# Four graph layers on one core: the bias of two banks written by ScalarE instead of PE, a copy moved to GpSimd, and a new order of the edge stages

## The reference, cut to what matters

```python
hi = x @ W1[:H];  hj = x @ W1[H:]
h = relu(hi[:, :, None, :] + hj[:, None, :, :] + b1)
y = h @ W2 + b2
y = layernorm(y) * gamma + beta
out = einsum('bij,bijh->bih', adj, y)
```

## Time and profile before

| | |
|---|---|
| median of 3 runs | 458.41 us (458.27 to 459.51) |
| profiled execution (the page gives its span) | 459.2 us |
| PE busy | 440.2 us, 96% |
| DVE busy | 416.2 us, 91% |
| ACT busy | 386.5 us, 84% |
| POOL busy | 354.0 us, 77% |
| granted TensorE clock, mean | 0.987 |

### The profile page before, as it was taken

The page is one execution under the profiler, slowest core; times in us unless marked ns, Lnnn a source line. Parts: engine busy times, 40 slices in busy tenths (PEclk is TensorE's granted clock), DMA queues, the critical chain, the costliest instruction groups (busy, mean ns, idle before and its releaser), DMA issues. The chain is left out here.

```text
span 459.2 us, 14175 instructions
## 1 busy us (share of the span) xinstructions
PE 440.2 (96%) x3420; PEld 414.6 (90%) x3453; DVE 416.2 (91%) x1523; ACT 386.5 (84%) x1003; POOL 354.0 (77%) x651
## 2 busy tenths in 40 slices
PE   8699989999999999999999999999999999999993
PEld 3599989999999999889998999999999999999991
DVE  6989999999999999996898898899889888989975
ACT  2368979999999899998788888888888888888874
POOL 4569979999999899756677787777768676868762
PEclk9889999999999999999999999999999999999997
DMA  7134344445444652233313222232223131313111
GB/s 221 41 83 131 95 139 161 153 151 178 154 148 156 221 190 77 76 109 121 122 55 99 69 74 80 69 85 63 91 60 94 51 103 51 103 51 86 37 46 49
DMA packets 50939, 47.60 MB, mean 104 GB/s; under 512 B 5584, under 2 KB 42576, under 8 KB 50896
## 3 DMA queue, kind: packets, MB, share of 16 engines
q1 hardware_dynamic: 49760, 46.45, 33.2%
q10 hardware_dynamic: 1136, 0.66, 0.5%
HBM read 28.22 MB, written 18.87 MB: 103 GB/s over the span
## 5 line engine op out<-in xcount | busy, mean ns | idle before, releaser
L1593 PEld LDWEIGHTS bank<-w2c,hE 128*128 128x128 f32 x512 | 67.3, 192 | 2.4
L1593 PE MATMUL bank<-w2c,hE 128*128 128x128 f32 x512 | 67.5, 275 | 0.2
L905 ACT ACTIVATE hE<-bank,front 128x512 f32<-128x512 f32 x64 | 44.2, 691 | 7.6 <-PE bank L1574 7.4
L927 ACT ACTIVATE sqE<-bank 128x512 f32<-128x512 f32 x63 | 37.7, 599 | 12.8 <-PE bank L1593 12.3
L1237 DVE TENSOR_REDUCE ssum<-sqE 128x4 f32<-128x512 f32 x63 | 42.6, 676 | 4.3 <-ACT sqE L927 2.9
L706 POOL TENSOR_TENSOR gHl<-gH,gHu 128x512 fp32r<-128x512 f32 x32 | 41.0, 1283 | 5.6 <-ACT gHu L879 5.6
L1104 DVE BATCH_NORM_STATS2 stats<-t 128x6 f32<-128x128 f32 x192 | 44.4, 272 | 1.0 <-issue 1.0
L1262 DVE TENSOR_TENSOR ym<-bank,wE 128x512 f32<-128x512 f32 x64 | 43.2, 681 | 1.6 <-POOL wE L755 0.3
L722 POOL TENSOR_TENSOR half<-ym 128x512 f32<-128x512 f32 x31 | 39.5, 1273 | 3.3 <-DVE ym L1262 3.1
L1591 PE MATMUL bank<-bias,ones_b 128*128 128x512 bf16 x92 | 35.0, 380 | 0.7 <-DVE ym L1262 0.6
L1593 PEld LDWEIGHTS bank<-w2c,hC 128*128 128x128 f32 x256 | 33.6, 192 | 1.3
(11 more groups left out here) (191 smaller groups left out, 1624.6 us busy)
## 6 DMA issues: line engine op xcount, KB each, us to landing
hh_scratch<-hh SPq DMA_DIRECT2D x32, 256.0 KB, 2.2
gH<-hh_scratch SPq DMA_DIRECT2D x32, 256.0 KB, 2.8
A<-adj_groups SPq DMA_DIRECT2D x32, 128.0 KB, 2.1
res_scratch<-res SPq DMA_DIRECT2D x32, 128.0 KB, 2.1
gRES<-res_scratch SPq DMA_DIRECT2D x32, 128.0 KB, 2.5
AT<-adjT_groups SPq DMA_DIRECT2D x31, 128.0 KB, 2.3
out<-y SPq DMA_DIRECT2D x30, 128.0 KB, 1.9
X<-x_groups SPq DMA_DIRECT2D x29, 128.0 KB, 2.2
```

The costliest lines, as they stand in the source:

```text
L905: nc.scalar.activation(hE[g][:, :], HE_ps, ACT.Relu, bias=C["L3_b1"]).then_inc(b[f"hE{g}_ready"], 1)
L927: nc.scalar.activation(sqE[g][:, :, :], YE_ps[g], ACT.Square).then_inc(b[f"sqE{g}_ready"], 1)
L1593: last = nc.tensor.matmul(ps[:, i, :], hidden[:, i * P:(i + 1) * P], w2c[:, :], start=False, stop=i == tiles - 1)
```

## The change

1. ScalarE writes the bias. For every unit but the first, a new stage `seed_ell(g)` (`sd0`, `sd1`) copies the centred bias row, repeated four times, into the bank of m0 or m1 as soon as `x0` or `x1` of the unit before has read it. `project` then leaves its product of ones and bias out, and its four products add to what is there. m0 and m1 wait for the seed instead of for `ymE0`, `ymE1`. `mc` keeps its product.
2. `split_upper` leaves ScalarE. GpSimd's `add_ends` (`hs`) does it as a `tensor_copy` behind its sum, and waits for one semaphore more (`HC_psum` of two units before).
3. SP's `next_h` is placed by `spl` alone. Its waits are as before.
4. `T3` and `FIRST` are new, `FIRST` now for units 0 to 7. The constants (`PERIOD3`, `AGES`, `START3`) are as before.

```diff
-        T3 = {"idx": 0, "T": 2.44, "spu": 3.82, "hs": 6.51, "beg": 7.08, "Qp": 7.27, "rows": 8.02, "spl": 8.21, "kS": 11.23, "V": 11.89,
-              "g0": 12.34, "T2": 14.04, "r0": 14.78, "cols": 15.16, "gc": 15.34, "kST": 15.55, "g1": 15.81, "rc": 16.63, "r1": 17.9,
-              "m0": 18.3, "mc": 19.24, "s0": 19.26, "m1": 19.31, "sqc": 20.27, "d0": 20.97, "s1": 21.21, "dc": 21.5, "d1": 23.51,
-              "std": 23.58, "rec": 24.31, "w": 25.33, "x0": 25.58, "yn": 25.84, "x1": 25.92, "a1": 28.54, "a2": 29.78, "sc": 31.11,
-              "tot": 33.56, "gm": 33.91, "rs": 34.76, "st": 35.78, "ag": 37.68, "fstd": 38.76, "frec": 41.49, "om": 43.47, "sh": 46.57,
-              "app": 49.01}
+        T3 = {"idx": 11.83, "rows": 19.84, "V": 25.63, "cols": 27.21, "g0": 24.24, "g1": 26.7, "gc": 27.9, "m0": 28.45, "m1": 32.1, "mc": 30.82,
+              "sc": 43.04, "Qp": 15.42, "kS": 18.49, "kST": 23.94, "r0": 21.32, "r1": 24.83, "rc": 24.3, "sd0": 24.05, "sd1": 25.41, "s0": 26.02,
+              "s1": 29.14, "sqc": 29.1, "std": 29.77, "fstd": 45.76, "app": 56.37, "beg": 16.18, "T": 11.05, "T2": 22.48, "d0": 28.62, "d1": 30.77,
+              "dc": 30.14, "rec": 32.25, "x0": 32.94, "x1": 34.86, "yn": 34.7, "tot": 41.42, "st": 44.67, "ag": 44.82, "frec": 53.11, "spl": 13.44,
+              "hs": 10.29, "a1": 33.48, "a2": 37.09, "gm": 39.87, "rs": 41.67, "w": 30.03, "om": 46.9, "sh": 50.85}
...
-            edge_stages = [(("idx", 0.5), next_ot), (("spl", "hs", 1.5), next_h), (("rs", 0.8), next_res), (("app", 1), store)]
+            edge_stages = [(("idx", 0.5), next_ot), (("spl", 1.5), next_h), (("rs", 0.8), next_res), (("app", 1), store)]
...
                 wait_past(pool, b["HE1_psum"], count(2))
+                wait_past(pool, b["HC_psum"], count(2))
                 nc.gpsimd.tensor_tensor(hs[q][:, :, :], gH[q][:, :, 0:P], gH[q][:, :, P:2 * P], ALU.add).then_inc(b["hs_ready"], 1)
+                nc.gpsimd.tensor_copy(gHu[q][:, :, :], gH[q][:, :, :]).then_inc(b["split_up"], 1)
...
-            def split_upper(q, u, count):
-
-                act.wait_ge(gh_loaded[q], (u - q) * 8 + 16)
-                wait_past(act, b["HE1_psum"], count(2))
-                wait_past(act, b["HC_psum"], count(2))
-                nc.scalar.activation(gHu[q][:, :, :], gH[q][:, :, :], ACT.Copy).then_inc(b["split_up"], 1)
...
+            def seed_ell(g):
+                def stage(q, u, count):
+                    if isinstance(u, int) and u == 0:
+                        return
+                    act.wait_ge(b[f"ymE{g}_ready"], count(1))
+                    nc.scalar.activation(YE_ps[g], b2c[:, :].unsqueeze(1).to_broadcast([P, ELL, P]), ACT.Copy).then_inc(b[f"seedE{g}_done"], 1)
+                return stage
...
-            edge_stages = [("spu", split_upper), ("Qp", keep_Q), ("kS", keep_S), ("kST", keep_ST), ("r0", hidden_ell(0)),
-                      ("r1", hidden_ell(1)), ("rc", hidden_csr), ("s0", square_ell(0)), ("s1", square_ell(1)),
+            edge_stages = [("Qp", keep_Q), ("kS", keep_S), ("kST", keep_ST), ("r0", hidden_ell(0)),
+                      ("r1", hidden_ell(1)), ("rc", hidden_csr), ("sd0", seed_ell(0)), ("sd1", seed_ell(1)), ("s0", square_ell(0)), ("s1", square_ell(1)),
...
-            def project(ps, hidden, tiles, done):
-                nc.tensor.matmul(run(ps), ones_b[:, :], run(bias3[:, :, :]), start=True, stop=False)
+            def project(ps, hidden, tiles, done, seeded=False):
+                if not seeded:
+                    nc.tensor.matmul(run(ps), ones_b[:, :], run(bias3[:, :, :]), start=True, stop=False)
...
-                    wait_past(pe, b[f"ymE{g}_ready"], count(1))
-                    project(YE_ps[g], hE[g], ELL, f"YE{g}_psum")
+                    seeded = not (isinstance(u, int) and u == 0)
+                    if seeded:
+                        pe.wait_ge(b[f"seedE{g}_done"], count(1))
+                    else:
+                        wait_past(pe, b[f"ymE{g}_ready"], count(1))
+                    project(YE_ps[g], hE[g], ELL, f"YE{g}_psum", seeded)
```

More of the change, by code:

```diff
@@ L305, in gnn_stack @@
                   "esd_ready", "erstd_ready", "wE_ready", "ymE0_ready", "ymE1_ready", "yC_ready", "O_psum", "half_done", "accE_ready",
[L306 removed]
+                  "tot_ready", "gout_done", "tout_ready", "ostats_done", "omv_ready", "omean_ready", "ostd_ready", "orstd_done", "oshift_ready", "out_ready", "seedE0_done", "seedE1_done"]
         b = {n: sem("u_" + n) for n in names3}
@@ L364, in wait_past @@
                 engine.wait_ge(semaphore, n)
-        T3 = {"idx": 0, "T": 2.44, "spu": 3.82, "hs": 6.51, "beg": 7.08, "Qp": 7.27, "rows": 8.02, "spl": 8.21, "kS": 11.23, "V": 11.89,
[4 rows of a table removed]
-              "app": 49.01}
+        T3 = {"idx": 11.83, "rows": 19.84, "V": 25.63, "cols": 27.21, "g0": 24.24, "g1": 26.7, "gc": 27.9, "m0": 28.45, "m1": 32.1, "mc": 30.82,
[4 rows of a table added]
         AGES = 4
         START3, EARLY, CATCH = 216.0, 5.0, 25.0
[L376 to L380, removed]
[7 rows of a table removed]
-                 ("beg", 2): 225.69, ("beg", 3): 240.58, ("beg", 4): 244.47, ("beg", 5): 247.21, ("rows", 0): 219.62, ("rows", 1): 225.56,
-                 ("rows", 2): 229.73, ("rows", 3): 243.06, ("rows", 4): 251.45, ("rows", 5): 263.45, ("s1", 0): 220.31, ("s1", 1): 234.83,
[4 rows of a table removed]
-                 ("cols", 0): 223.8, ("cols", 1): 228.19, ("cols", 2): 236.96, ("cols", 3): 246.55, ("cols", 4): 261.85, ("cols", 5): 272.97,
-                 ("gc", 0): 224.76, ("gc", 1): 229.1, ("gc", 2): 238.28, ("gc", 3): 247.38, ("gc", 4): 261.99, ("gc", 5): 274.28, ("kST", 0): 225.01,
-                 ("kST", 1): 228.65, ("kST", 2): 242.85, ("kST", 3): 249.8, ("kST", 4): 262.68, ("kST", 5): 273.1, ("rc", 0): 226.69,
[5 rows of a table removed]
-                 ("std", 3): 262.55, ("std", 4): 275.09, ("std", 5): 281.29, ("rec", 0): 229.34, ("rec", 1): 239.04, ("rec", 2): 246.8,
[9 rows of a table removed]
-                 ("fstd", 3): 281.1, ("frec", 0): 268.55, ("frec", 1): 276.47, ("frec", 2): 280.71, ("frec", 3): 281.94, ("om", 0): 271.08,
-                 ("om", 1): 276.44, ("om", 2): 277.25, ("sh", 0): 271.19, ("sh", 1): 277.18, ("sh", 2): 280.73, ("app", 0): 272.51,
-                 ("app", 1): 277.83, ("app", 2): 281.76}
@@ new lines, in gnn_stack @@
+        FIRST = {("Qp", 0): 219.14, ("Qp", 1): 223.36, ("Qp", 2): 227.15, ("Qp", 3): 239.84, ("Qp", 4): 248.55, ("Qp", 5): 258.4, ("Qp", 6): 274.66,
[7 rows of a table added]
+                 ("app", 0): 272.04, ("app", 1): 281.03, ("app", 2): 291.91, ("app", 3): 315.54, ("app", 4): 322.1, ("app", 5): 328.86,
+                 ("app", 6): 361.82, ("app", 7): 369.52, ("beg", 0): 219.43, ("beg", 1): 222.03, ("beg", 2): 223.3, ("beg", 3): 232.31,
+                 ("beg", 4): 251.52, ("beg", 5): 253.24, ("beg", 6): 265.36, ("beg", 7): 271.45, ("cols", 0): 224.52, ("cols", 1): 229.38,
+                 ("cols", 2): 238.08, ("cols", 3): 253.44, ("cols", 4): 259.97, ("cols", 5): 263.82, ("cols", 6): 265.46, ("cols", 7): 323.54,
[4 rows of a table added]
+                 ("frec", 3): 303.18, ("frec", 4): 320.46, ("frec", 5): 328.43, ("frec", 6): 356.15, ("frec", 7): 370.96, ("fstd", 0): 259.68,
+                 ("fstd", 1): 272.97, ("fstd", 2): 286.37, ("fstd", 3): 286.89, ("fstd", 4): 288.39, ("fstd", 5): 299.92, ("fstd", 6): 304.87,
[6 rows of a table added]
+                 ("idx", 0): 202.48, ("idx", 1): 222.5, ("idx", 2): 225.64, ("idx", 3): 229.54, ("idx", 4): 242.35, ("idx", 5): 251.6,
+                 ("idx", 6): 264.74, ("idx", 7): 286.45, ("kS", 0): 221.75, ("kS", 1): 226.94, ("kS", 2): 232.11, ("kS", 3): 248.24,
+                 ("kS", 4): 255.95, ("kS", 5): 266.42, ("kS", 6): 274.59, ("kS", 7): 315.9, ("kST", 0): 224.97, ("kST", 1): 229.45,
+                 ("kST", 2): 243.71, ("kST", 3): 253.68, ("kST", 4): 259.52, ("kST", 5): 277.74, ("kST", 6): 281.07, ("kST", 7): 310.48,
[8 rows of a table added]
+                 ("rec", 0): 229.59, ("rec", 1): 241.95, ("rec", 2): 251.34, ("rec", 3): 258.85, ("rec", 4): 278.5, ("rec", 5): 290.01,
+                 ("rec", 6): 293.58, ("rec", 7): 305.83, ("rows", 0): 219.42, ("rows", 1): 225.78, ("rows", 2): 230.46, ("rows", 3): 248.15,
+                 ("rows", 4): 254.04, ("rows", 5): 266.61, ("rows", 6): 323.47, ("rows", 7): 342.37, ("rs", 0): 254.44, ("rs", 1): 265.21,
[8 rows of a table added]
+                 ("sh", 7): 381.89, ("spl", 0): 212.28, ("spl", 1): 221.28, ("spl", 2): 228.44, ("spl", 3): 247.3, ("spl", 4): 252.43,
+                 ("spl", 5): 258.97, ("spl", 6): 262.62, ("spl", 7): 288.41, ("sqc", 0): 227.82, ("sqc", 1): 233.9, ("sqc", 2): 247.71,
+                 ("sqc", 3): 256.6, ("sqc", 4): 266.48, ("sqc", 5): 279.07, ("sqc", 6): 281.76, ("sqc", 7): 296.61, ("st", 0): 249.28,
+                 ("st", 1): 265.56, ("st", 2): 284.91, ("st", 3): 303.95, ("st", 4): 305.18, ("st", 5): 359.28, ("st", 6): 359.77, ("st", 7): 385.7,
```

(10 more changed lines are left out.)

## The result

The changed kernel takes 453.4 us in the median of 4 runs (452.92 to 454.56); the kernel before took 458.74 beside it (458.27 to 459.51). The ratio is 0.988, 95% interval 0.9857 to 0.9902. Forecast were 446.8, range 443 to 457. The direction was right and the time lies in the range; the gain is 5.3 us instead of 11.6, less than half.

A forecast was written before the change was run, and what follows sets the result against it. PE was taken as the bound, its period falling from 7.80 to 7.38 us: 10.1 over 24 units, 1.1 in units 1 to 5, 0.4 in the last two, total 11.6 from 458.4, giving 446.8 us, range 443 to 457.

The forecast's parts named there:

- PE bounds and two products go: Repeating part: PE bounds nearly all; two of three bias products leave it, 0.22 us each, 7.74 to 7.31 a unit.
- I let +0.08 and -0.08 cancel, and keep 7.22 to 7.40 for PE: PE's unit: one type switch fewer at m1 offsets m0's first weight load behind idx's short products; 7.31 us stays.
- Units 1 to 5 ... half taken ... 1.1: Passage out of the dense part: two products fewer per unit, 2.15 us, half credited as a gain of 1.1.
- a longer passage: Sign that the forecast is wrong altogether: the new starting order, written out for eight units, lengthens the passage; no size given.
- Units 30 and 31, -0.4: Last two units: products gone save 0.86 us, half credited as 0.4; stages behind m1 of unit 31 unchanged.
- Seed 0.55, room of 0.2 in the ring: ScalarE's seed takes 0.55 us; one unit's chain of waits through it sums to 7.09, 0.2 under PE's 7.31.
- Loop end 0.3 or less at yn: VectorE's loop end, moved behind x0 and tot, shows an "issue" gap at yn of 0.3 us or less.
- Copy 1.0, bounds 0.74 to 1.28: GpSimd's 512-element copy takes 1.0 us, between a 256-element two-input sum (0.74) and a 512-element subtraction (1.28).
- the rival of the other side: GpSimd becomes the bound, with 7.21 us of work plus remaining waits; period 8.2, time 468 us; chance 0.14.
- Base: Starting time: profiled span 459.2 us, run median 458.41, 0.8 less; the forecast's differences are taken from the median.
- the own range of the sum: Periods of 7.25 to 7.60 us, with 1.5 more and one either way, give 443 to 453 us.
- a ring or loop end as the bound: Rival: the chain of waits through the seed, or VectorE's loop end, bounds; period 7.56 to 7.7, 454 us; chance 0.17.

## Why the prediction was wrong

- *PE bounds and two products go*: right. No waits of PE after, 34 bias products as forecast, and 0.22 a product confirmed by leaving out mc's.
- *"I let +0.08 and -0.08 cancel, and keep 7.22 to 7.40 for PE"*: this step failed, the term of PE's work was too small. PE's work is 7.475, out of its range. The order costs 0.11 (unit 7.85 with products, with GpSimd's copy or without it, against 7.74), mostly g1 behind the fp32 products of sc; and m0 without its bias product takes 0.06 more. The hoped saving at mc to m1 isn't there: that pitch is still 0.89 (348.08 to 348.97). The period was forecast 7.38 and is 7.478: 24 units gave 8.0 instead of 10.1.
- *"Units 1 to 5 ... half taken ... 1.1"*: failed, the largest term, +1.9 instead of -1.1. The products taken by themselves do bring 1.3 (old order without bias). The copy on GpSimd and the new order each cost about as much again (1.3 and 1.1), and the products that go turn into PE's idle time there (120.45 with them, 120.39 without). One piece is traced, PE's 0.84 for AD behind the copy. The prediction named a longer passage at its end as what would upset it and gave it no term, although the diff showed that copy and order both change it.
- *Units 30 and 31, -0.4*: failed, found +0.3 (24.73 to 25.03 behind unit 29; the two units 14.71 in place of 14.43). The products by themselves bring 1.1 there (23.65 on the old order), but the new order with them takes 25.06, and with the seeds 25.03. The prediction took this end as untouched by the order.
- *Seed 0.55, room of 0.2 in the ring*: right in outcome. 600 ns busy, and the seed at 346.16 is followed by the next start at 346.68, 0.52. In the repeating part the seeds cost nothing, as the run without them shows. The room is as small as forecast, 0.17 between the seed's end and m0, and the sum of the ring was made for one order only: on the old one PE waits for the seed in almost every unit.
- *Loop end 0.3 or less at yn*: right, 0.26. In the wrong place it costs 0.6 a unit.
- *Copy 1.0, bounds 0.74 to 1.28*: 0.62, below my lower bound. A sum of 256 elements with two inputs is no lower bound for a copy of 512 with one. The Trainium skill (GPSIMD Engine Reference, section 3.1) gives 769 ns, as measured in the best case of a tight loop over 512 elements; the rows here say 620, and the measurement decides. GpSimd as the bound, the rival of the other side, doesn't occur: 6.41 a unit. But the same cheap copy costs 0.17 a unit and 1.3 in the passage on the old order.
- *Base*: by all runs the time is the span plus 1.8, so the profiled execution of before had 461.0, not 459.2. 1.75 of the 2.6 by which this exceeds the median is the late clock between 20 and 30 us. The differences were taken from 458.4 and are not touched by it.

The missing 6.6 us: 3.0 in the passage, 2.1 in the 24 units, 0.7 at the end, and 0.8 that the sum leaves (458.4 less 5.75 is 452.7, measured 453.4; 0.3 of it is that the kernel before took 458.74 beside this one). That the time still lies in the stated range owes something to luck: the own range of the sum ended at 453, and the part from there to 457 was added for a ring or loop end as the bound, and neither binds.

What stays open: which single waits of the passage could be had back. Moving one T only handed the time on, and hs of unit 0 behind the scaling of AD, where the kernel before has it, was not run by itself. No version here with the bias kept beats the changed kernel beyond the intervals.

## What to carry to other kernels

Where one engine bounds with no waits, a new order has a price of its own on that engine: add up the pitches in the new neighbourhoods before crediting what was removed. A stage between two others may look misplaced by its own pitch and be the cover for a result on its way; ask what it hides before moving it. And a part written out by hand for other engines' loads (a passage) needs its own term in the sum, with idle time, not only fewer instructions.

## What the hardware showed

- A 128x512 copy from SBUF into a bank on ScalarE takes 600 ns busy with the next start 0.52 later, against 625 ns for the copy into SBUF.
- The first product of a gather takes 0.25 to 0.27 to the next start behind fp32 products and 0.17 to 0.18 behind fp32r ones. m0 takes 0.95 straight behind the bf16 products of idx or rows and 0.89 behind a bias product, and mc straight behind m0's fp32 products 0.89. Why, no run here settles.
- The end of a loop trip on VectorE shows 1.07 us behind two short reciprocals, 1.17 behind one (VectorE 0.8 later), 0.47 or 0.26 behind x0 and tot.
